# Zeroing expert slots beside the first norm and projection, and storing the output sequence by sequence

## The reference

```python
x = L0_attn_x
xn = _layernorm(x, axis=-1)
x = x + _L0_attn_ref(xn, ...) + _L0_ffn_ref(xn, ...)
xn = _layernorm(x, axis=-1)
x = x + _L1_attn_ref(xn, ...) + _L1_ffn_ref(xn, ...)
xn = _layernorm(x, axis=-1)
x = x + _L2_attn_ref(xn, ...) + _L2_ffn_ref(xn, ...)
xn = _layernorm(x, axis=-1)
x = x + _L3_attn_ref(xn, ...) + _L3_ffn_ref(xn, ...)
return x
```

## Time and profile before

| | |
|---|---|
| median of 3 runs | 2432.92 us |
| lowest and highest run | 2426.63, 2435.71 us |
| span of the profiled execution | 2426.4 us |
| its mean granted TensorE clock | 0.898 |
| busy share PE, DVE, ACT, POOL | 82%, 72%, 49%, 22% |
| DMA bytes | 155.90 MB, mean 64 GB/s |

### The profile page before, as it was taken

The page is one execution under the profiler, slowest core; times in us unless marked ns, Lnnn a source line. Parts: engine busy times, 40 slices in busy tenths (PEclk is TensorE's granted clock), DMA queues, the critical chain, the costliest instruction groups (busy, mean ns, idle before and its releaser), DMA issues. The chain is left out here.

```text
span 2426.4 us, 45617 instructions
## 1 busy us (share of the span) xinstructions
PE 2000.9 (82%) x17760; PEld 1033.8 (43%) x17760; DVE 1737.1 (72%) x2865; ACT 1197.8 (49%) x2434; POOL 536.6 (22%) x640
## 2 busy tenths in 40 slices
PE   2788876975739999999689879988799788797898
PEld 1222221632302349633343348845544345555554
DVE  4999998667789985698555953355666697766665
ACT  2999998233408872478533223325433021075433
POOL 1111110014954431244302521125300000001100
PEclk8798999987659999899878989989899899988999
DMA  7423320001724227332100122201123433000000
GB/s 235 102 53 88 70 53 1 0 17 46 195 80 105 51 62 211 74 68 43 21 8 18 40 69 89 93 30 38 42 72 99 145 88 91 4 5 26 1 1 35
DMA packets 146774, 155.90 MB, mean 64 GB/s; under 512 B 53004, under 2 KB 122315, under 8 KB 146563
## 3 DMA queue, kind: packets, MB, share of 16 engines
q1 hardware_dynamic: 131912, 119.78, 18.7%
q0 software_dynamic: 12928, 25.47, 4.1%
q10 hardware_dynamic: 1728, 7.87, 0.8%
HBM read 87.37 MB, written 68.55 MB: 64 GB/s over the span
## 5 line engine op out<-in xcount | busy, mean ns | idle before, releaser
L428 ACT ACTIVATE a_E<-a_scores,a_nmax 128x512 f32<-128x512 f32 x512 | 343.7, 796 | 15.8 <-DVE a_nmax L361 15.1
L1002 ACT ACTIVATE a_E<-a_scores 128x512 f32<-128x512 f32 x512 | 273.3, 600 | 108.9 <-PE a_scores L1037 92.3
L361 DVE TENSOR_REDUCE a_nmax<-a_scores 128x2 f32<-128x1024 f32 x256 | 302.6, 1217 | 22.8 <-PE a_scores L443 18.7
L906 DVE TENSOR_REDUCE a_nmax<-a_first 128x2 f32<-128x1024 f32 x256 | 296.8, 1217 | 22.9 <-PE a_first L1027 20.7
L443 PE MATMUL a_scores<-a_Vh,a_Kh 48*128 48x512 bf16 x512 | 108.4, 421 | 95.4 <-ACT a_E L428 71.1
L456 PE MATMUL a_turn<-a_E,a_QS 128*32 128x256 f32 x2048 | 175.9, 420 | 2.5 <-DVE a_QS L371 2.2
L1037 PE MATMUL a_scores<-a_Qh,a_Kh 51*128 51x512 bf16 x512 | 165.1, 400 | 11.4 <-PEq L50 4.9
L1027 PE MATMUL a_first<-a_Kh,a_Qh 48*128 48x512 bf16 x512 | 148.7, 418 | 30.5 <-DVE a_nmax L906 15.9
L1059 PE MATMUL a_out<-a_E,a_V 128*32 128x256 f32 x2048 | 164.0, 400 | 0.2 <-issue 0.2
L428 ACT ACTIVATION_READ_ACCUMULATOR a_E<-a_scores,a_nmax 128x1 f32 x512 | 157.6, 316 | 0.0
L443 PEld LDWEIGHTS a_scores<-a_Vh,a_Kh 48*128 48x128 bf16 x512 | 24.9, 94 | 217.0 <-ACT a_E L428 178.5
(11 more groups left out here) (499 smaller groups left out, 4581.6 us busy)
## 6 DMA issues: line engine op xcount, KB each, us to landing
f_up<-in_L_up SPq DMA_DIRECT2D x32, 256.0 KB
slots<-zeros ACTq DMA_DIRECT2D x12, 640.0 KB, 15.0
a_Kh<-a_rows_k SPq DMA_DIRECT2D x16, 384.0 KB, 5.9
a_Vh<-a_rows_v SPq DMA_DIRECT2D x16, 384.0 KB, 8.8
a_Qh<-a_rows_q SPq DMA_DIRECT2D x32, 192.0 KB
a_Kh<-a_rows_k SPq DMA_DIRECT2D x32, 192.0 KB
f_xe<-slots SPq DMA_DIRECT2D x40, 128.0 KB, 2.1
outs<-f_ye POOLq DMA_DIRECT2D x40, 128.0 KB, 2.0
```

Source lines behind the costliest of these rows:

```text
L361: v.tensor_reduce(nmax[:, rd % 2, r1, :, q], bank(b, u)[:], AX.X, ALU.max, negate=True).then_inc(S["max_ready"], 1)
L428: m = a.activation(E[:, u % NE, x], bank(b, u)[:, x], ACT.Exp, bias=nmax[:, rd % 2, r1, x, q:q + 1], accum_out=Z[:, rd % 2, r1, x, q:q + 1])
L906: v.tensor_reduce(out, slot_bank(n)[:], AX.X, ALU.max, negate=True).then_inc(S["slot_read"], 1)
L1002: a.activation(E[:, u % NE, x], ps_s[n % 3][:], ACT.Exp, scale=SCALE).then_inc(S["exp_ready"], 1)
```

## The change

The twelve stores of zeros leave ScalarE's queue in the opening block and go to SP: the eight of `slots2` in the block of the first norm, the four of `slots1` at the head of the block of the first projection, ahead of SP's wait for `parts_ready`. Behind these four SP also issues the load of `ln_cols`, which gets a semaphore of its own, and the three weights of the first feed-forward part. The opening block waits for the identity alone. The output is stored by SP inside the last block of f3, in eight DMAs of 256 KB, each when the third `added` of its sequence is set; the separate last block is gone.

```diff
-def attention0(nc, g, w):
+def attention0(nc, g, w, ahead):
...
                 @block.sync
                 def _(sp):
+                    ahead(sp)
                     sp.wait_ge(S["parts_ready"], 1)
...
             def load_weights(sp):
+                sp.wait_ge(g.ln_cols_loaded, 16)
                 sp.dma_start(W[:], w["L3_mix"]).then_inc(mix_loaded, 16)
...
+        stored = g.sem("f3e_stored")
         with nc.Block() as block:
+            @block.sync
+            def _(sp):
+                sp.wait_ge(g.slots_zeroed, 16 * 12)
+                for b in range(NB):
+                    sp.wait_ge(S["added"], 3 * b + 3)
+                    sp.dma_start(out_rows[:, b], g.X[:, b].rearrange("p r c -> p (r c)")).then_inc(stored, 16)
+                sp.wait_ge(stored, NB * 16)
...
                 sp.dma_start(g.ident[:], w["identity"]).then_inc(loaded, 16)
-                sp.dma_start(g.ln_cols[:], w["L3_ln"]).then_inc(loaded, 16)
...
-                for t, n in zip(g.f0_weights, ("L0_wgT", "L0_wuT", "L0_wdT")):
-                    sp.dma_start(t[:], w[n]).then_inc(g.f0_loaded, 16)
-                sp.wait_ge(loaded, 32)
+                sp.wait_ge(loaded, 16)
 
             @block.scalar
             def _(a):
                 a.wait_ge(zeroed, 1)
-                for rows in (g.slots1, g.slots2):
-                    flat = rows.rearrange("(p n) c -> p (n c)", p=128)
-                    for i in range(flat.shape[1] // 1280):
-                        a.dma_start(flat[:, i * 1280:(i + 1) * 1280], zeros[:]).then_inc(g.slots_zeroed, 16)
                 a.activation(g.unit_root[:], zeros[:, 0:1], ACT.Sqrt)
+
+        def zero_rows(sp, rows):
+            flat = rows.rearrange("(p n) c -> p (n c)", p=128)
+            for i in range(flat.shape[1] // 1280):
+                sp.dma_start(flat[:, i * 1280:(i + 1) * 1280], zeros[:]).then_inc(g.slots_zeroed, 16)
+
+        def beside_first_norm(sp):
+            zero_rows(sp, g.slots2)
+
+        def beside_first_projection(sp):
+            zero_rows(sp, g.slots1)
+            sp.dma_start(g.ln_cols[:], w["L3_ln"]).then_inc(g.ln_cols_loaded, 16)
+            for t, n in zip(g.f0_weights, ("L0_wgT", "L0_wuT", "L0_wdT")):
+                sp.dma_start(t[:], w[n]).then_inc(g.f0_loaded, 16)
+
         run = {
-            "ln0": lambda: layer_norm(nc, g, "0", g.X, g.XN, g.XT, by_row=True),
-            "a0": lambda: attention0(nc, g, w),
+            "ln0": lambda: layer_norm(nc, g, "0", g.X, g.XN, g.XT, by_row=True, ahead=beside_first_norm),
+            "a0": lambda: attention0(nc, g, w, beside_first_projection),
...
-        stored = g.sem("stored")
-        with nc.Block() as block:
-            @block.sync
-            def _(sp):
-                sp.wait_ge(g.slots_zeroed, 16 * 12)
-                sp.dma_start(out.rearrange(x_rows, r=R), g.X[:].rearrange("p b r c -> p b (r c)")).then_inc(stored, 16)
-                sp.wait_ge(stored, 16)
```

More of the change, by code:

```diff
@@ L2513, in layer2, with ffn3 @@
         g.sems += k.sems
-def ffn3(nc, g, w):
+def ffn3(nc, g, w, out_rows):
     NT = NB * R
@@ L2619, in ffn3, with experts3 @@
             layer_norm(nc, g, "3b", g.XN, rows, HT, scale=ln_cols[:, 2:3], bias=ln_cols[:, 3:4], by_row=True)
-        experts3(nc, g, weights, weights_loaded, SG, HT)
-def experts3(nc, g, weights, weights_loaded, SG, HT):
+        experts3(nc, g, weights, weights_loaded, SG, HT, out_rows)
+def experts3(nc, g, weights, weights_loaded, SG, HT, out_rows):
     NF = 4
@@ L3667, in build @@
         g.f0_loaded = nc.alloc_semaphore("f0_loaded")
+        g.ln_cols_loaded = nc.alloc_semaphore("ln_cols_loaded")
         zeros = first.sb("zeros", [128, 1280])
@@ L3716, in build @@
             "a3": lambda: attention3(nc, g, w),
-            "f3": lambda: ffn3(nc, g, w),
+            "f3": lambda: ffn3(nc, g, w, out.rearrange(x_rows, r=R)),
         }
```

## The result

The changed kernel took 2414.2 us (median of 4 runs, 2411.96 to 2421.80) against 2429.78 us for the kernel before (4 runs). The ratio is 0.9933, with a 95% interval of 0.9907 to 0.9959: 16.3 us faster, between 10 and 23. The forecast was 13.1 us off a median of 2432.92. Of the 5.6 us between 2419.8 and 2414.2, 3.1 are the fourth run of the kernel before, which moved its median to 2429.78.

A forecast was written before the change was run, and what follows sets the result against it. Only the ends count: the opening waits for DMA engines moving zeros, the close for one 2048 KB output store. Gains 7.3 + 0.8 + 0 + 0 + 5.0 = 13.1 us off 2432.92 give 2419.8 us, range 2416 to 2427.

The forecast's parts named there:

- Step 1: Opening: loads of x without zeros beside them run at 385 GB/s; the norm starts at 11.4, 7.3 us earlier.
- the 1.2 us that I held possible: Opening: loss from the 7.3 us if SP's issues stay slow and the block ends at 11.5.
- Rival (a): Opening: x is read no faster than 215 to 300 GB/s; time 2421.1 to 2423.4; chance 0.14.
- Step 2: First projection: it no longer waits for its weights, which land right behind x; 0.8 us gained.
- Steps 3 and 4: Norm (eight stores of zeros) and projection (four, plus loads): SP's issues and zeros cost nothing; late spill up to 3 us.
- (b): First norm: eight slow SP issues hold its block open by 4 us; time 2423.8; chance 0.11.
- (c): First spill: zeros not through when it goes out, by 2 to 5 us; time 2421.8 to 2424.8; chance 0.12.
- (d): First spill: zeros on SP's queue run at 215 GB/s, spill 16.5 us late; time 2436.3; chance 0.04.
- Step 5: Close: output by sequences, only the last store counts, landing in 2.6 us; 5.0 us gained, bounds 4.2 and 5.3.
- rival (e): After the opening: earlier work meets TensorE's clock change at another point; 3 us either way; chance 0.09 as deciding thing.
- Two of the signs: Prediction wrong if the spill's wait exceeds 24.1 us, or anything between 80 and 2380 us changes by over 3 us.

The follow-up runs named there:

- late_zeros: Changed kernel with all twelve stores of zeros moved behind the last rows of attention 0; trace only, second norm's statistics at 435.56 us.
- norm12: Changed kernel with all twelve stores of zeros beside the first norm; trace only, projection started at 25.44 us, 4.4 us later.
- twice_zeros: Changed kernel with eight stores of zeros beside the projection, not four; trace only, TensorE's wait for the rows grew from 24.9 to 29.8 us.
- gap1: Changed kernel with the projection held back by a 1024-column memset on VectorE; trace only, 64.7 us from norm to a reciprocal in attention 0.
- gap1_warm: gap1 with six products of the identity filling TensorE's pause before the projection; trace only, 62.6 us from norm to a reciprocal in attention 0.
- weights_first: Kernel before with the seven weights of attention 0 issued ahead of x; trace only, 64.8 us from norm to a reciprocal in attention 0.
- warm_scores: Changed kernel with 32 and 18 unread products filling TensorE's pause until the first rows are back; ratio 1.0023 to the kernel before.
- warm_short: warm_scores with the products cut to 13 and 8; ratio 0.9936 to the kernel before.
- before_again: Kernel before, unchanged, executed once more for its profile; trace only, 65.7 us from norm to a reciprocal in attention 0.
- front_only: Changed kernel with only the new opening, the output stored by one DMA at the end; ratio 0.9951 to the kernel before.
- after_again: Changed kernel, unchanged, timed a second time; ratio 0.9936, 2422.67 against 2437.72 us for the kernel before.
- store_only: Kernel before with only the output stored by sequences, the opening as before; ratio 0.9965 to the kernel before.
- wait_only: Kernel before without SP's wait for the column loads (`ln_cols`) in the opening block; trace only, norm started at 19.26 us, projection at 30.43.
- x8: Changed kernel with x loaded in eight DMAs of one sequence, not four of two; ratio 0.9944 to the kernel before.

## Why the prediction was wrong

**Step 1** was right on the zeros and nearly in size: norm 7.6 us earlier, forecast 7.3. x came at 385 GB/s and more without zeros beside it, the last load had landed at 8.8 us (forecast 8.9), and SP's issues took 0.43 to 0.5 us each, so none of the 1.2 us that I held possible was lost. Rival (a) is out. But what bounds the end of the statistics is another thing than I had: not the last load and the four statistics behind it (8.9 + 1.42 = 10.3), but all sixteen, 5.54 us of VectorE behind the first landing, ended at 10.23. That the two give the same is luck.

**Step 2** was right: 0.98 us, forecast 0.8.

**Steps 3 and 4** were right: late_zeros shows a cost of nothing, and norm12 and twice_zeros what it would have been otherwise. The margins were thinner than stated: an issue took 1.24 us and not 0.63, which left SP 0.9 us instead of 3.9 in the norm. The queue was empty at 33 to 34 us, as worked out (33.3). Rivals (b), (c) and (d) did not come about.

**Step 5** was right in mechanism and undersized: 5.6 us, forecast 5.0. The landing was the term that was mis-sized: the 256 KB store landed in 2.0 us (at most 2.4), where I had 2.6, and below the 2.3 us of the nearest row.

**The step that failed is rival (e)** and its place in the sum. I saw that TensorE's clock in the opening could change, and gave it "a few us either way", with a mean of nothing. The traces show 12.0 us at norm 2 for the opening (11.0 in the pair before and after alone) against the 8.1 of steps 1 to 4. In the means of the four old and the three new openings the norm starts 7.6 us earlier, 1.1 us is the wait in step 2, and the sum put four more terms at nothing: 1.8 us less from projection to first spill, 1.2 less from first scores to mark, 0.9 less from mark to norm 2, and 0.6 more for rows that came back more slowly. The first two go with the low clock: it lies in the projection in three of the four old openings and in none of the three new ones, and it lasts until 19 us into the scores in two of the old and in none of the new ones. In before itself the projection had the full clock, and the 2.6 us were lost in the scores. Whether the wait of step 2 brings the low clock into the projection is made likely by gap1 and gap1_warm, and not shown, since weights_first, warm_scores and warm_short have it without the wait. Why it lasts longer in the scores of before, before_again, weights_first and twice_zeros is open. The 0.9 us between mark and norm 2 I can't ascribe.

**The starting point** was off too: 2432.92 us was the median of three runs, and with the fourth it is 2429.78. The same working from there gives 2416.7 us and a range that begins at 2412.9, which holds 2414.2. The time fell 1.8 us below the range; this 3.1 us would explain it without the clock, and the times can't tell the two apart. It is the traces that show the clock's part.

The sum of the parts as measured is 12.0 + 5.6 = 17.6 us (16.6 in the pair), forecast 13.1; the times say 16.3 and 15.6 with intervals of 5 us and more to each side.

Two of the signs that I had named came: TensorE's wait for the rows grew from 24.14 to 24.88 us, though not by the zeros (late_zeros), and the stretch from norm 2 to the last addition changed by more than 3 us, from 1971.8 to 1982.2.

What stays open: why the clock fell in weights_first and in the two kernels with added products, though TensorE rested only 1.5 us; and whether the stretch from norm 2 to the last addition is quite untouched. It took between 1951 and 1992 us in the traces, with jumps where low stretches lie; in front_only, for one, the windows over the norm and routing of layer 1 (491 to 557 us) had a clock of 0.51. But it isn't without order: in the traces that were taken together, four groups with both openings, it was longer with the new one in three (after 1982.2 against 1971.8; after_again and front_only 1984.3 and 1992.3 against store_only and wait_only 1975.2 and 1975.0; gap1 and x8 1957.0 and 1960.5 against before_again and weights_first 1951.5 and 1956.8) and the same in the fourth (gap1_warm 1974.9 against 1975.1 and 1974.3). If some of the 12 us were lost again behind norm 2, these traces would look so; the timed front_only, 11.9 us with an interval of 5 to 19, can't exclude it.

## What to carry to other kernels

Stores that nobody waits for still take DMA time from loads at the head of a kernel: give them a place where the DMA engines are idle, and count what each costs the queue that issues it, since a block lasts as long as its slowest issuer. Store the output piece by piece, so that only the last piece is seen. When whole runs scatter more than the edit is worth, compare the start of one instruction in several traces close behind the edit; here that told 12 us within 1.4, where two spans said 6. What happens behind that instruction it can't tell. Before giving a low clock a price, look which engine sets the pace while it lasts.

## What was unexpected of the hardware

A DMA issue on SP took 0.33 to 0.5 us with little queued and 1.2 to 1.3 us behind stores of zeros, whichever transfer it was for; in wait_only, with zeros issued by ScalarE beside it, up to 1.9 us. A pause of TensorE that was 1.4 us longer went with 3.3 us lost, 1.3 of them in a projection at half clock and 0.8 behind the first scores, where the low clock lasted longer. The full clock in the first 4 to 5 us of the first scores was worth nothing, beside ScalarE and VectorE; each us by which the low clock lasted longer than 13 us cost some 0.4 us.
